# Splitting one more product of the token loop into half-precision parts, and reordering the attention stage

## The reference

```python
# x: 64 x 64 frames of 75 nodes and 3 channels; three graph layers 3 -> 128 -> 128 -> 64
x = einsum('btvc,co->btvo', x, W); x = einsum('uv,btvo->btuo', A, x)   # one layer,
x = (x + b - m) * (g * rsqrt(v + 1e-5)) + be                           # relu after the first two
h = mean over the 75 nodes                                             # tokens, 64 x 64 x 64
h = concatenate([h, txt], axis=1)                                      # 64 x 96 x 64
h = h + attention(layernorm(h))     # Q, K, V with biases, softmax(Q K^T / 8) V
z = layernorm(h)
for _ in range(30):
    z = z + 0.01 * tanh(z); z = z * sigmoid(z); z = layernorm(z) * w + b; z = z @ W.T + bias
h = h + z
```

## Time and profile before

| | |
|---|---|
| time, median of 3 runs | 1561.95 us (1561.27 to 1564.09) |
| profiled execution | 1566.86 us, its span 1565.0 us |
| mean granted PE clock | 0.986 of full |
| busy share of the span | PE 96%, PEld 74%, DVE 87%, ACT 74%, POOL 80% |
| token loop | about 75 to 1105 us of the span |
| attention | about 1114 to 1184 us |

### The profile page before, as it was taken

How to read it: one execution, slowest core, us unless ns; L and a number is a source line. 1 busy time by engine, 2 the same in 40 slices (tenths; PEclk the granted TensorE clock), 3 DMA queues, 4 the chain that set the end, 5 groups by cost and what they waited for, 6 DMA issues and landing times. The chain is left out here.

```text
span 1565.0 us, 64358 instructions
## 1 busy us (share of the span) xinstructions
PE 1506.1 (96%) x22398; PEld 1162.8 (74%) x22398; DVE 1364.2 (87%) x3311; ACT 1154.8 (74%) x2707; POOL 1255.3 (80%) x1309
## 2 busy tenths in 40 slices
PE   8499999999999999999999999999895999999998
PEld 8477777777777777777777777777684888888887
DVE  6388888888888888888888888888778999999998
ACT  3377778777777777777787777777345887787876
POOL 2288888888888888888888888888676888888887
PEclk9999999999999999999999999999986999999999
DMA  5300000000000000000000000001021000000001
GB/s 117 101 9 8 8 8 7 7 8 8 7 7 8 8 8 7 7 8 8 7 7 7 8 8 7 7 8 26 4 53 28 0 0 0 0 0 0 0 0 41
DMA packets 21672, 21.68 MB, mean 14 GB/s; under 512 B 12255, under 2 KB 19343, under 8 KB 21272
## 3 DMA queue, kind: packets, MB, share of 16 engines
q1 hardware_dynamic: 19482, 19.28, 4.6%
q0 software_dynamic: 1120, 1.44, 0.4%
q10 hardware_dynamic: 1044, 0.64, 0.2%
HBM read 14.43 MB, written 6.92 MB: 14 GB/s over the span
## 5 line engine op out<-in xcount | busy, mean ns | idle before, releaser
L725 DVE SCALAR_TENSOR_TENSOR y<-ps,negb,abar 128x375 f32<-128x375 f32 x820 | 459.3, 601 | 94.7 <-PE ps L625 94.6
L679 POOL TENSOR_TENSOR y0lo<-y_whole,y0hi 128x384 f16<-128x384 f32 x410 | 374.6, 914 | 166.1 <-ACT y_whole L653 151.5
L603 PE MATMUL ps<-AThi,y0hi 64*128 64x150 f16 (+1 forms) x4920 | 434.3, 217 | 3.5 <-POOL y0lo L679 3.4
L603 PE MATMUL ps<-AThi,y0lo 64*128 64x150 f16 (+1 forms) x4920 | 434.9, 215 | 0.0
L603 PE MATMUL ps<-ATlo,y0hi 64*128 64x150 f16 (+1 forms) x4920 | 434.6, 214 | 0.0
L688 POOL TENSOR_TENSOR y<-y 128x370 f32<-128x370 f32 x410 | 400.0, 976 | 2.1 <-DVE y L725 1.9
L651 ACT ACTIVATE y0hi<-ps 128x384 f16<-128x384 f32 x410 | 202.7, 494 | 235.9 <-POOL y0lo L679 220.6
L1309 POOL TENSOR_TENSOR rs<-var,expo 128x8 f32<-128x8 f32 x180 | 313.5, 1752 | 52.0 <-DVE var L1376 52.0
L625 PE MATMUL ps<-z_whole,W1s 128*128 128x375 f32 x820 | 313.7, 504 | 0.0
L660 ACT ACTIVATE z_whole<-ps 128x375 f32<-128x375 f32 x615 | 268.5, 493 | 1.4 <-PE ps L603 1.4
L713 DVE SCALAR_TENSOR_TENSOR y0lo<-ps,y0hi 128x384 f16<-128x384 f32 x410 | 226.4, 552 | 19.5 <-ACT y0hi L651 19.1
(11 more groups left out here) (191 smaller groups left out, 2377.4 us busy)
## 6 DMA issues: line engine op xcount, KB each, us to landing
z_static<-z_rows SPq DMA_DIRECT2D x410, 18.0 KB
xs<-in_x_v SPq DMA_DIRECT2D x5, 720.7 KB, 9.2
z_rows<-zp SPq DMA_DIRECT2D x10, 240.0 KB
h_rows<-h SPq DMA_DIRECT2D x16, 96.0 KB, 1.8
h2r<-h_rows SPq DMA_DIRECT2D x6, 256.0 KB, 2.7
out<-h2r SPq DMA_DIRECT2D x6, 256.0 KB, 2.3
z_rows<-zp POOLq DMA_DIRECT2D x5, 240.0 KB, 3.1
h<-in_txt SPq DMA_DIRECT2D x1, 512.0 KB, 4.5
```

Source lines behind the costliest of these rows:

```text
L603: last = nc.tensor.matmul(ps[:, Z1B + 2 * p + j, f0 * V:f0 * V + w], y[rows, par, p, t * C:(t + 1) * C], a[rows, BAND0[t]:BAND0[t] + w], s ...
L679: nc.gpsimd.tensor_tensor(y0lo[:, par, p, 0:HC], y0f[:, p, :], y0hi[:, par, p, 0:HC], ALU.subtract).then_inc(y0lo_by_pool, 1)
L725: nc.vector.scalar_tensor_tensor(y1[:, par, 2 * p + i].rearrange("p f v -> p (f v)"), ps[:, Y1B[p][i], 0:GV], negb1[:, 0:1], abar[:].rearr ...
```

## The change

In the token loop the second quarter (p = 0, i = 1) gets the treatment of the first: ACT writes a second half-precision copy, POOL subtracts to get its remainder, and layer1 does three half-precision products instead of one in fp32. POOL's second fold (L691) goes, and DVE sums 380 elements for both pairs. Several waits of PE that others imply are left out.

In attention, the query and key projections, whose 128 x 128 weights hold the same 64 x 64 block twice on the diagonal, are done as two 64 x 64 products each, in opposite quarters of the array and into the same bank. The order within a step changes: on PE from AV, SC, PT, QKV, HT to SC, QKV, AV, HT, PT; on ACT the copy prT moves from the head to behind hT; on DVE the scaling of group t-4 moves from the head to behind val.

```diff
@@ layer0, PE
-                    pe.wait_ge(zst_loaded[par], loads * (2 * 16))
+                    if p == 0 or isinstance(it, int) and it == 0:
+                        pe.wait_ge(zst_loaded[par], loads * (2 * 16))
@@ mix, PE
-                    pe.wait_ge(y0lo_by_pool, n + 1)
-                    pe.wait_ge(y0lo_by_dve, n + 1)
...
+                    if p == 1 or not late(it, 1):
+                        pe.wait_ge(y0lo_by_pool, n + 1)
+                    if p == 1 and late(it, 1):
+                        pe.wait_ge(y1_done[1], unit(it - 1, 0) + 1)
@@ layer1, PE, p == 0
-                        nc.tensor.matmul(ps[:, Y1B[0][1], 0:GV], W1s[:], z1f[:, par, 0, :], start=True, stop=True).then_inc(y1_ready[1], 1)
+                        for i in range(2):
+                            pe.wait_ge(z1lo_done[i], it + 1)
+                            o = ps[:, Y1B[0][i], 0:GV]
+                            nc.tensor.matmul(o, W1hi[:], z1hi[:, par, i, :], start=True, stop=False)
+                            nc.tensor.matmul(o, W1hi[:], z1lo[:, par, i, :], start=False, stop=False)
+                            nc.tensor.matmul(o, W1lo[:], z1hi[:, par, i, :], start=False, stop=True).then_inc(y1_ready[i], 1)
@@ z1_high, ACT, after the z1f copies
+                    if p == 0:
+                        nc.scalar.activation(z1hi[:, par, 1, :], ps[:, Z1B + 1, 0:GV], ACT.Identity).then_inc(z1hi_done, 1)
@@ POOL, between y0_low(it + 1, 1 - par, 0) and halve(it - 1, 1 - par, 0)
+                def z1_low(it, par):
+                    pool.wait_ge(z1hi_done, it * 2 + 2)
+                    nc.gpsimd.tensor_tensor(z1lo[:, par, 1, :], z1f[:, par, 0, :], z1hi[:, par, 1, :],
+                                            ALU.subtract).then_inc(z1lo_done[1], 1)
@@ halve, POOL
-                    if p == 0:
-                        pool.wait_ge(halved, n + 1)
-                        nc.gpsimd.tensor_tensor(y[:, :, U2:V], y[:, :, U2:V], y[:, :, U1:U2], ALU.add).then_inc(quartered, 1)
@@ pool_nodes, DVE, both pairs
+                    dve.wait_ge(halved, unit(it, p) + 1)
+                    nc.vector.tensor_reduce(pooledT[:, 2 * p:2 * p + 2, bass.ds(it * GF, GF)], y1[:, par, 2 * p:2 * p + 2, :, U1:V],
+                                            AX_X, ALU.add).then_inc(pooled[p], 1)
@@ attention, PE, on(1)
-                    last = nc.tensor.matmul(ps[:, QK, i * GP * S:(i + 1) * GP * S], w,
-                                            hT[:].rearrange("p g s -> p (g s)"), start=True, stop=True)
+                    for half in halves:
+                        last = nc.tensor.matmul(ps[half, QK, i * GP * S:(i + 1) * GP * S], w[half, half],
+                                                hT[half].rearrange("p g s -> p (g s)"), start=True, stop=True)
```

More of the change, by code:

```diff
@@ L510, in tokenise @@
         y0f = sb("y0_whole", [P, PAIRS, HC])
-        z1hi = sb("z1hi", [P, 2, GV], F16)
-        z1lo = sb("z1lo", [P, 2, GV], F16)
+        z1hi = sb("z1hi", [P, 2, 2, GV], F16)
+        z1lo = sb("z1lo", [P, 2, 2, GV], F16)
         z1f = sb("z1_whole", [P, 2, QUART - 1, GV])
@@ L522, in tokenise @@
         z1hi_done = sem("z1hi_done")
-        z1lo_done = sem("z1lo_done")
+        z1lo_done = [sem("z1lo_by_dve"), sem("z1lo_by_pool")]
         z1f_done = sem("z1_whole_done")
@@ L533, in tokenise @@
         LAST = GROUPS - 1
-        U1, U2 = V // 2, V // 2 + (V - V // 2) // 2
+        U1 = V // 2
         def steps(eng, body):
@@ L584, in layer0, with mix @@
                     last.then_inc(y0_ready, 1)
-                def mix(it, par, p):
+                def mix(it, par, p, last_one):
                     n = unit(it, p)
-                    pe.wait_ge(y0lo_by_pool, n + 1)
-                    pe.wait_ge(y0lo_by_dve, n + 1)
-                    if late(it, 1):
-                        if p == 0:
[L593 to L597, removed]
+                    if last_one:
+                        pe.wait_ge(y0lo_by_dve, n + 1)
+                    if p == 1 or not late(it, 1):
+                        pe.wait_ge(y0lo_by_pool, n + 1)
+                    if p == 1 and late(it, 1):
+                        pe.wait_ge(y1_done[1], unit(it - 1, 0) + 1)
                     for t in range(CHUNKS):
@@ L612, in layer1 @@
                     if p == 0:
-                        pe.wait_ge(z1lo_done, it + 1)
                         pe.wait_ge(z1f_done, it * 3 + 3)
[L615 to L618, removed]
-                        nc.tensor.matmul(ps[:, Y1B[0][1], 0:GV], W1s[:], z1f[:, par, 0, :], start=True, stop=True).then_inc(y1_ready[1], 1)
+                        for i in range(2):
[4 more added lines that the diff above has]
+                            nc.tensor.matmul(o, W1lo[:], z1hi[:, par, i, :], start=False, stop=True).then_inc(y1_ready[i], 1)
                     else:
                         for i in range(2):
-                            pe.wait_ge(z1f_done, it * 3 + 2 + i)
-                            if late(it, 1):
+                            if isinstance(it, int) and it == LAST:
+                                pe.wait_ge(z1f_done, it * 3 + 2 + i)
                                 pe.wait_ge(y1_done[i], n - 1)
@@ L634, in body @@
                         layer0(it + 1, 1 - par, 0, pair + 2)
-                    mix(it, par, 0)
-                    mix(it, par, 1)
+                    mix(it, par, 0, last)
+                    mix(it, par, 1, last)
                     if not last:
@@ L657, in z1_high @@
                     if p == 0:
-                        nc.scalar.activation(z1hi[:, par, :], ps[:, Z1B, 0:GV], ACT.Identity).then_inc(z1hi_done, 1)
+                        nc.scalar.activation(z1hi[:, par, 0, :], ps[:, Z1B, 0:GV], ACT.Identity).then_inc(z1hi_done, 1)
                     for i in range(1 - p, 2):
@@ L698, in body @@
                         y0_low(it + 1, 1 - par, 0)
+                    z1_low(it, par)
                     if late(it, 1):
@@ L716, in z1_low @@
                 def z1_low(it, par):
-                    dve.wait_ge(z1hi_done, it + 1)
-                    nc.vector.tensor_tensor(z1lo[:, par, :], ps[:, Z1B, 0:GV], z1hi[:, par, :], ALU.subtract).then_inc(z1lo_done, 1)
+                    dve.wait_ge(z1hi_done, it * 2 + 1)
+                    nc.vector.tensor_tensor(z1lo[:, par, 0, :], ps[:, Z1B, 0:GV], z1hi[:, par, 0, :], ALU.subtract).then_inc(z1lo_done[0], 1)
                 def weigh(it, par, p, i):
@@ L1074, in tensor @@
     def tensor(pe, token):
+        halves = [slice(0, D), slice(D, 2 * D)]
         def body(t, on):
[L1076 to L1084, removed]
             if on(2):
@@ L1094, in body @@
                 last.then_inc(score_ready, 1)
[L1095 to L1102, removed]
             if on(1):
@@ L1115, in body @@
                 last.then_inc(val_ready, 1)
+            if on(4):
+                g = t - 4
+                pe.wait_ge(prT_done, g + 1)
+                if not isinstance(g, int) or g >= 1:
+                    pe.wait_ge(av_done, g)
+                for i, j in enumerate(ORDER):
+                    last = nc.tensor.matmul(ps[0:S, AV, j * D:(j + 1) * D], prT[:, i, :], val[:, bass.ds(g * GB + j, 1), :].rearrange("p one d -> p (one d)"),
+                                            start=True, stop=True)
+                last.then_inc(av_ready, 1)
             if on(0):
@@ L1124, in body @@
                 last.then_inc(hT_ready, 1)
+            if on(3):
+                g = t - 3
+                pe.wait_ge(exp_done, g + 1)
+                if not isinstance(g, int) or g >= 1:
+                    pe.wait_ge(prT_done, g)
+                for j in range(GB):
+                    last = nc.tensor.transpose(ps[0:S, PT, j * S:(j + 1) * S], pr[:, j, :], ident[0:S, 0:S])
+                last.then_inc(prT_ready, 1)
         steps(pe, body, token)
@@ L1128, in body @@
         def body(t, on):
[L1129 to L1133, removed]
             if on(1):
@@ L1144, in body @@
                                      ACT.Identity).then_inc(hT_done, 1)
+            if on(3):
+                g = t - 3
+                act.wait_ge(prT_ready, g + 1)
+                nc.scalar.activation(prT[:].rearrange("p b s -> p (b s)"), ps[0:S, PT, 0:GB * S],
+                                     ACT.Identity).then_inc(prT_done, 1)
             if on(2):
@@ L1155, in body @@
         def body(t, on):
[L1156 to L1161, removed]
             if on(2):
@@ L1185, in body @@
                                  ALU.add).then_inc(val_done, 1)
+            if on(4):
+                g = t - 4
+                dve.wait_ge(av_ready, g + 1)
+                dve.wait_ge(inv_done, g + 1)
+                v_.tensor_tensor(h2[:, grp(g), :], ps[0:S, AV, 0:GB * D].rearrange("p (b d) -> p b d", d=D),
+                                 spread(inv[:, grp(g)], S, GB), ALU.mult).then_inc(av_done, 1)
             if on(3):
```

2 lines of the change are left out of this document (removed).

## The result

The changed kernel takes 1553.52 us in the median of 4 runs (1551.9 to 1555.69), the kernel before 1562.34 beside it (4 runs). The ratio is 0.9943 with a 95% interval of 0.9926 to 0.9961: faster, by 8.8 us (0.6%). The forecast was 1547, 15 us faster; the range holds the result. The profiled execution took 1555.69 us, its span 1553.9.

What follows compares the result with a forecast made beforehand. PE was taken to bound the token loop, with DVE's evictions late next. The loop's 18 us less and attention's 3 us more gave -15, so 1561.95 became 1547 us, range 1531 to 1564.

Steps and rivals of the forecast that it cites:

- PE's work in a step: Token loop: three half-precision products replace one fp32 product, saving 0.16 us, so PE alone needs 4.87 instead of 5.03.
- The turn: Token loop, PE: the change to 64-row tiles ahead of layer0, taken to cost 0.09 us after half-precision products too.
- What is late next: Token loop: DVE's evictions become late, and two rings through them set the step at 4.94 us.
- ring 1: Token loop, one step: PE's mix for p = 1 through DVE's evictions to the next such mix, 4.93 us (4.89 to 4.99).
- ring 2: Token loop, over two steps: through ACT's eight operations, DVE's evictions and back on PE, 9.88 us, so 4.94 a step.
- The rest of the loop: Token loop: added work on ACT, POOL (subtraction 0.89 us) and DVE stays hidden, the sums barely, by about 0.1 us.
- case 4: Rival, token loop: POOL and DVE take back the gain, period again 5.03, 1562 to 1565 us; chance 0.10.
- The query and key products: Attention: the quarters of a pair run together, adding only one turn of the tile shape, 0.09 to 0.2 us.
- rival 2: Attention: query and key pairs serialise in one PSUM bank, 10 us longer, 1554 us in all; chance 0.15.
- The new order: Attention: a ring over two steps closes through POOL's addition, 7.4 us against 7.07, so 3 us more over 8 pairs.
- Case 3: Rival, attention: gaps keep PE at half clock, 12 more steps at 1.9 us each, 1570 us; chance 0.10.
- The bound of -5: Attention, lower bound of its change: another order may spare PE two steps at half clock, 5 us less.

Runs made afterwards that it cites:

- e11: e7 with DVE's last eviction of a token step doing 3 of its 5 frames, the rest left out: 1527.12 us, ratio 0.9753.
- e12: e7 with two half-precision products of layer1 for p = 0 left out on PE: 1533.76 us, ratio 0.9796.
- e4: The new token loop with attention in the old order, but query and key products in quarters: 1549.52 us, ratio 0.9909 to the kernel before.
- e3: The changed kernel with full query and key products instead of quarters, attention in the new order: 1554.22 us, ratio 0.9943 to the kernel before.
- e7: e1 with POOL's addition in attention one step later: 1541.88 us, ratio 0.9855 to the kernel before.
- e8: The changed kernel, all of it, with POOL's addition in attention one step later: 1542.14 us, ratio 0.9853 to the kernel before.
- e5: The changed kernel with DVE's scaling in attention back at the head of its step: 1571.31 us, ratio 1.0049 to the kernel before.
- e1: The changed kernel with attention as it was before, so only the token loop changed: 1547.88 us, ratio 0.9909 to the kernel before.

## Why the prediction was right, and where it was off

- **PE's work in a step.** Right. The turn costs about 0.1 after half-precision products too, and PE alone needs 4.88 (e11) against 4.87. That leaves nothing for the waits left out, which were costed at nothing.
- **What is late next.** Right: 4.938 against 4.94. The two rings are separable: ring 1 is 4.89 (e12; I had 4.93, the hand-over of 0.10 being too long, 0.06 measured), ring 2 is 9.88 for two steps, and shows as steps of 4.99 and 4.89 in turn. So ring 2 alone sets 4.94, and that the two rings "agree" was no support. That ring 2 came out to 0.01 is in part luck: its hand-over to PE was 0.04 too long as well and its eight ACT operations take 2.94 instead of 2.98, while y0hi and its hand-over take 0.61 instead of 0.55 (608.44 to 609.05) and the way back on PE 3.71 instead of 3.69. The 202 steps give 18.3 us against 18.
- **The rest of the loop.** The subtraction takes 0.90 against 0.89. "Hidden, but barely" came out as worked out: DVE's sum waits for the fold, 50.9 us in all, and the sums still end 0.09 ahead of the first weigh, where I had 0.1. But the sign written down for case 4, DVE's sum waiting for POOL's fold, could not tell case 4 from the forecast: the wait appeared and case 4 didn't. That a wait appears doesn't make it the bound.
- **The query and key products.** Right that the pairs run together, so rival 2 falls: the rule quoted there (the Trainium skill, TensorEngine Tiling (Array Packing), Gotcha 1) names row tiles, and does not hold for these quarters, which lie in different rows and in different columns of the array: 0.80 us measured against 1.3 if they took turns. The turns cost more than the 0.09 to 0.2 taken in the old order, 0.29 a step in e4, as both edges of QK and that of V pay; in the new order it is 0.12 (QK to V 0.80 against 0.75, V to AV 0.51 against 0.44 in e3).
- **The new order.** This is the step that failed in size, and for most of the 6.5 us by which the median missed: +3 us forecast for attention, +7.5 measured (+14 was the bound). First, the pair itself. I summed the ring through ACT's copy of hT, 0.33 and its hand-overs. On PE, however, PT and SC stand between the transposes and QK, and everything up to AV follows in order: 1133.11 to 1136.40, 3.29 us, where I had 2.81. DVE then comes to the scaling only at 1137.12, 0.72 after AV's end, where I took some tenths for one step of two; in this pair the feed-forward's statistics (L1374) stand ahead of it too. POOL's part, 1129.36 to 1133.06, is 3.70 as forecast. The sum, 3.70 + 0.05 + 3.29 + 0.72 + 0.41 + 0.08, is 8.25, where I had 7.04 and took 7.4 for two steps; without the statistics pairs take 7.59 and 8.30. Second, and larger: the forecast multiplied one pair by eight, and had no term for the last part of the stage, where the feed-forward's powers (L1285) join rstd on POOL and the new order makes PE wait 3.3 us for the next norm (1142.98). About 5.5 of the 7.5 us arise there. e7 and e8 cut the ring at the addition, and the loss is gone. e7 also corrects the reading of the earlier trace rows: without the wait for the scaling its pair at full clock is 7.09 (additions at 1113.50 and 1120.59), as before, so in the old order that wait on POOL did not set the pair.
- **Clock.** The granted clock is 0.50 in 1155 to 1160 and 0.56 in 1160 to 1165 after, against 0.50 in the last windows before. Case 3 didn't happen: the low stretch moved and did not grow by steps (mean granted clock of the stage 0.89 after, 0.86 before). Its price of 5.43 for a step does not isolate the clock: PE's own work fills that step at half clock, but in e8 at a granted clock of 1.00 POOL's norms stand as far apart where both powers come between them (1132.98 and 1138.41). The bound of -5 was mis-sized too: two steps at 1.9 are 3.8. In e5, where PE waits in every step, the stage's clock is 0.85.
- **The feed-forward.** Nothing was forecast, 1.2 us came, within the spread of the same code in the other profiles; whether it has a cause stays open.

## What to carry to other kernels

Before costing a saving on the busiest engine, sum the rings that pass through it and through the next one: here the rings gave 4.94 where the engine alone would have given 4.87, and the ring that doesn't contain the saved work is the floor. Draw a ring with each engine's whole queue in it: what matters is not what an instruction depends on, but what its engine does first. When an in-order engine mixes old work that waits (the addition) with new work that others wait for (the norms), let the old work lag one step more; here that was worth 12 us in the new order and 6 in the old one (e1 to e7). And when a sum is one period times a count, look whether the period holds in every part of the stage.

## What the runs showed of the hardware that I had not expected

That two 64 x 64 products in opposite quarters of the array run together into one bank was forecast; no run had shown it before (0.80 us against about 1.3). ACT's records lengthen along an unbroken row of operations: in the kernel after y0hi goes from 0.49 (605.50) to 0.58 (608.44) and y0f to 0.60 (609.18), while an operation still starts every 0.37; the queue's pace, not the length of a record, is what a sum needs.
